# Moving the values' projection and the keys' transposes in the TensorE order of a linear-attention and low-rank FFN block

## The reference

```
xn  = layernorm(layernorm(x))*ln_g + ln_b          # attention: second norm with weights
q, k, v = split(xn @ W_qkv + b_qkv)
gate = sigmoid(layernorm(x) @ W_gate + b_gate);  gate = gate / (mean(gate) + EPS)
q = relu(q*gate)**2 + EPS;   k = relu(k*gate)**2 + EPS
out_t = (q_t . sum_{s<=t} k_s v_s^T) / (q_t . sum_{s<=t} k_s + EPS)      # per head
x = x + out @ W_proj + b_proj
P = layernorm(x) @ U1;  H = gelu(P @ V1 + b1);  x = x + (H @ U2) @ V2 + b2   # rank 128, width 2048
```

## Time and profile before

| | us |
|---|---|
| median of 3 runs (lowest, highest) | 1736.85 (1735.19, 1737.18) |
| the profiled execution's own time | 1734.75 |
| its span in the profile | 1733.0 |
| PE busy in the span | 1703.1 (98%) |
| DVE busy | 1340.5 (77%) |
| POOL busy | 894.4 (52%) |
| ACT busy | 671.5 (39%) |

### The profile page before, as it was taken

One profiled execution on the slowest core, in us unless ns is written; L12 is line 12 of the kernel. 1 busy time (PEld: TensorE's weight loads), 2 busy tenths in 40 slices (PEclk: granted clock), 3 DMA queues, 4 the chain that ended last, 5 costly groups with the idle time before them and its releaser, 6 DMA issues.

```text
span 1733.0 us, 39458 instructions
## 1 busy us (share of the span) xinstructions
PE 1703.1 (98%) x16477; PEld 1429.5 (82%) x16477; DVE 1340.5 (77%) x2159; ACT 671.5 (39%) x1242; POOL 894.4 (52%) x1026
## 2 busy tenths in 40 slices
PE   6999999999999999999999999999999999999997
PEld 4788888888888888888888888888888888888886
DVE  6877877777877777777778778778777778777775
ACT  4243343443433343433433434434333434334333
POOL 4365555555555545555555555555555555555540
PEclk9999999999999999999999999999999999999999
DMA  7111111111011111110111110111111111101100
GB/s 220 59 35 53 34 53 40 33 53 53 33 53 33 41 53 40 46 53 23 52 53 34 53 44 30 53 53 33 53 39 36 53 41 45 53 23 52 41 20 26
DMA packets 61937, 82.09 MB, mean 47 GB/s; under 512 B 14952, under 2 KB 25600, under 8 KB 61760
## 3 DMA queue, kind: packets, MB, share of 16 engines
q1 hardware_dynamic: 60896, 77.99, 14.3%
q10 hardware_dynamic: 864, 1.57, 0.3%
HBM read 62.60 MB, written 16.94 MB: 46 GB/s over the span
## 4 chain that ended last, share of the span: by engine, by line
PE 95%; DVE 3%; ACT 0%; issue 0%; DMA 0%; POOL 0%; SPq 0%; DVEq 0%; POOLq 0%
PE ps_a L825 11%; PE ps_a L826 10%; PE ps_a L827 10%; PE scores L825 8%; PE scores L827 7%; PE scores L826 7%; PE ps_h L825 6%; PE scores L832 5%; PE ps_h L826 4%; PE ps_h L827 4%; PE scores L960 4%; PE scores L995 4%; PE ps_q L825 3%; PE ps_q L827 3%; PE ps_q L826 3%; PE scores L989 2%
## 5 line engine op out<-in xcount | busy, mean ns | idle before, releaser
L432 POOL TENSOR_TENSOR h_lo<-h_full,h_hi 128x512 fp32r<-128x512 f32 x244 | 334.1, 1379 | 194.7 <-DVE h_hi L654 194.7
L825 PE MATMUL ps_a<-wx_hi,zt_hi 128*128 128x512 f32 x768 | 312.7, 407 | 6.3 <-DVE key_sums L765 4.2
L827 PE MATMUL ps_a<-wx_hi,zt_lo 128*128 128x512 f32 x768 | 305.2, 397 | 0.0
L826 PE MATMUL ps_a<-wx_lo,zt_hi 128*128 128x512 f32 x768 | 305.2, 397 | 0.0
L515 ACT ACTIVATE h_full<-ps_h,cols 128x256 f32<-128x256 f32 x512 | 213.6, 472 | 21.2 <-PE ps_h L827 19.5
L654 DVE CAST h_hi<-h_full 128x512 fp32r<-128x512 f32 x256 | 173.8, 698 | 39.7 <-ACT h_full L515 39.7
L452 POOL TENSOR_TENSOR key_lo<-keys,key_hi 128x512 fp32r<-128x512 f32 x64 | 83.3, 1301 | 191.4 <-ACT key_hi L550 191.4
L825 PEld LDWEIGHTS ps_a<-wx_hi,zt_hi 128*128 128x128 f32 x768 | 145.8, 190 | 39.0 <-DVE zt_lo L609 7.1
L827 PEld LDWEIGHTS ps_a<-wx_hi,zt_lo 128*128 128x128 f32 x768 | 145.3, 189 | 35.5
L526 ACT ACTIVATE query_t<-scores 128x512 f32<-128x512 f32 x64 | 38.3, 598 | 346.2 <-PE scores L832 346.2
L720 DVE TENSOR_TENSOR probs<-scores,causal 128x2048 f32<-128x2048 f32 x64 | 146.7, 2292 | 32.5 <-PE scores L960 32.5
(11 more groups left out here) (158 smaller groups left out, 4225.6 us busy)
## 6 DMA issues: line engine op xcount, KB each, us to landing
xs<-L_attn_x SPq DMA_DIRECT2D x64, 256.0 KB, 4.0
out<-x1s SPq DMA_DIRECT2D x64, 256.0 KB, 2.1
xt<-x_turned SPq DMA_DIRECT2D x63, 256.0 KB, 4.2
key_sums<-carry_rows SPq DMA_DIRECT2D x60, 256.0 KB, 3.8
rows<-turned_rows SPq DMA_DIRECT2D x63, 64.0 KB, 4.4
x1s<-L_attn_W_gate SPq DMA_DIRECT2D x4, 256.0 KB, 4.1
x1s<-L_ffn_U SPq DMA_DIRECT2D x4, 256.0 KB, 6.5
carry_rows<-key_sums SPq DMA_DIRECT2D x64, 2.0 KB
```

Source lines behind the costliest of these rows:

```text
L432: E.tensor_tensor(h_lo[:, i % SLOTS, :], h_full[:, i % SLOTS, :], h_hi[:, i % SLOTS, :].bitcast(F32), ALU.subtract).then_inc(s["h_lo_ready ...
L825: E.matmul(ps, wh, mh, start=start and i == 0, stop=False)
L826: E.matmul(ps, wh, ml, start=False, stop=False)
L827: mm = E.matmul(ps, wl, mh, start=False, stop=stop and i == last)
```

## The change

Three things move. On PE the transposes of the keys leave their place behind QUERY, where they turned the keys of c; now they turn the keys of n, a step ahead, behind the product of probabilities and values, and write to `ps_a` instead of `ps_t`. VALUE comes directly behind the scores in both kinds of step; in an odd step the first FFN product used to stand between them. Behind VALUE or around it the FFN products are regrouped in twos: in an odd step pairs 0 and 1 stand between VALUE and the state's update, and pairs 2 and 3 behind the key transposes; in an even step pairs 4 and 5 stay ahead of the scores and 6 and 7 stand behind the key transposes. The key sums move behind pair 3 (or 7). ACT's and DVE's lists follow.

```
                 if n.exists:
                     pe.wait_ge(s["gate_evac"], n.done())
                     project(QUERY, ps_a, s["query_done"])
-                if c.exists:
-                    if d.exists:
-                        pe.wait_ge(s["x1t_ready"], d.done())
-                    else:
-                        pe.wait_ge(s["query_t_ready"], c.done())
-                    pe.wait_ge(s["key_ready"], c.done())
-                    transpose4(keys[:, c.half, :], s["tk_done"])
...
                     pe.wait_ge(s["key_t_ready"], c.done())
+                    pe.wait_ge(s["query_t_ready"], c.done())
+                    if d.exists:
+                        pe.wait_ge(s["x1t_ready"], d.done())
...
                     mm.then_inc(s["scores_done"], 1)
-                if ffn.exists and b % 2:
-                    h_pair(ffn, pairs[0])
                 if n.exists:
...
                     project(VALUE, ps_a, s["value_done"])
+                if ffn.exists and b % 2:
+                    h_pair(ffn, pairs[0])
+                    h_pair(ffn, pairs[1])
...
                     mm.then_inc(s["ot_done"], 1)
+                if n.exists:
+                    pe.wait_ge(s["value_ready"], n.done())
+                    pe.wait_ge(s["key_ready"], n.done())
+                    transpose4(keys[:, n.half, :], s["tk_done"], ps_a)
                 if ffn.exists:
-                    h_pair(ffn, pairs[1 if b % 2 else 2])
+                    h_pair(ffn, pairs[2])
+                    h_pair(ffn, pairs[3])
                 if n.exists:
-                    pe.wait_ge(s["value_ready"], n.done())
+                    pe.wait_ge(s["key_t_ready"], n.done())
                     pe.wait_ge(s["key_lo_ready"], n.done())
                     E.matmul(ps_a[:, :], causal_r[:, :], key_hi[:, :], start=True, stop=False)
                     E.matmul(ps_a[:, :], causal_r[:, :], key_lo[:, :], start=False, stop=True)\
                         .then_inc(s["sums_done"], 1)
-                if ffn.exists:
-                    if b % 2:
-                        h_pair(ffn, pairs[2])
-                    h_pair(ffn, pairs[3])
```

More of the change, by code:

```diff
@@ L538, in step @@
                         .then_inc(s["x1t_hi_ready"], 1)
-                if c.exists:
-                    act.wait_ge(s["tk_done"], c.done())
-                    E.activation(key_t[:, :, :].rearrange(flat), ps_t[:, :], ACT.Copy)\
-                        .then_inc(s["key_t_ready"], 1)
                 if b % 2 and ffn.exists:
@@ L551, in step @@
                 if ffn.exists:
-                    gelu(ffn, pairs[0 if b % 2 else 1])
+                    if b % 2:
+                        gelu(ffn, pairs[0])
+                    gelu(ffn, pairs[1])
                 if c.exists:
@@ L556, in step @@
                         .then_inc(s["ot_hi_ready"], 1)
+                if n.exists:
+                    act.wait_ge(s["tk_done"], n.done())
+                    E.activation(key_t[:, :, :].rearrange(flat), ps_a[:, :], ACT.Copy)\
+                        .then_inc(s["key_t_ready"], 1)
+                if ffn.exists:
+                    gelu(ffn, pairs[2])
                 z_head(Chunk(p, b + 1))
                 if ffn.exists:
-                    if b % 2:
-                        gelu(ffn, pairs[1])
-                    gelu(ffn, pairs[2])
                     gelu(ffn, pairs[3])
@@ L746, in step @@
                                     ALU.add).then_inc(s["state_ready"], 1)
+                if ffn.exists and b % 2:
+                    h_head(ffn, pairs[1], finishing)
                 if c.exists:
```

21 lines of the change are left out of this document (10 added, 11 removed).

## The result

| | before | after |
|---|---|---|
| median of 5 runs each (lowest, highest), us | 1736.85 (1735.19, 1737.46) | 1726.7 (1723.25, 1727.78) |
| the profiled execution's own time | 1734.75 | 1725.1 |
| its span | 1733.0 | 1723.4 |

What follows compares the result with a forecast made beforehand. PE bounds the kernel, busy 1703.1 of 1733.0 us. Bubbles 4.8, switches 0, last step 2.7 and first steps 0.6 make 8.1 us off 1734.75, 1726.7; the median lies 2.1 above, 1728.8, range 1721.5 to 1738.

Steps and rivals of the forecast that it cites:

- The bubble: Odd step, last FFN product waiting for the gelu two products before: this gap of 0.15 to 0.16 us goes, 4.8 us.
- The switch from tiles to transposes: Transposes directly behind the tiled products: the switch costs 0.10 us, so the swap is worth 0 per step.
- rival (a): The switch from tiles to transposes is free, or the clock holds: 6.2 or 1.2 us more gain, to 1721.4; chance 0.15.
- The last step: Last step with scores: two FFN products fill the wait for x1t_lo, scores start 2.2 to 3.3 us earlier, taken as 2.7.
- the case at half clock: Last step: the two FFN products take 2.8 us, so the scores start at 1693.2, the 2.2 us end of the gain.
- The first steps: Scores of the third step can go earlier, less 0.25 us paid in the second waiting for key_t: 0.6 us gained together.
- The clock at the start: Work behind PE's 4.2 us wait may leave half clock: 1.2 us at most, left out of the sum, in the range.
- `value_ready` 0.2 to 1.0 us ahead of its need: Even step: DVE's values end 0.2 to 1.0 us before the transposes behind the product of probabilities need them.
- Rival (c): POOL's key_lo precedes DVE's queries operation, value_ready is late in 31 even steps: 15.5 us less 8.1, 1744; chance 0.17.
- Key sums' chain, x1t, ot: Key sums have 0.6 us to spare for key_t, ot is done before the output projection, the x1t_ready wait can only shrink.
- P's halves get a whole projection more: Odd step: P's halves, which the first FFN product just met, get a whole projection more time with VALUE earlier.

Runs made afterwards that it cites:

- regroup_only: The changed kernel with the transposes of keys back behind QUERY, in bank ps_t: 1731.6 us, ratio 0.9973 to the kernel before.
- gelu_first: The kernel before with the odd step's second gelu and its cast taken ahead of zt, PE's list untouched: 1740.38 us, ratio 1.0027.
- warm: The changed kernel with matmuls that nobody reads filling PE's waits at the start and in the last step with scores: 1724.61 us, ratio 0.9940.
- joined_warm: The changed kernel with the edits of joined and warm together: 1724.47 us, ratio 0.9938 to the kernel before.
- one_pad: The changed kernel with only an unused buffer of 32 bytes per partition ahead of zt_hi: 1718.29 us, ratio 0.9901 to the kernel before.
- delay2: The changed kernel with two unread DVE operations ahead of values in each even step, their buffer shifting later ones by 64 bytes: 1727.4 us, ratio 0.9955.
- value_back: The changed kernel with the odd step's VALUE back behind the first FFN product: 1737.09 us, ratio 1.0008 to the kernel before.
- pads_on_after: The changed kernel with 32 unused bytes ahead of zt_hi and 32 more ahead of x1t_hi: 1709.35 us, ratio 0.9851 to the kernel before.
- joined: The changed kernel with the even step's transposes of queries moved directly ahead of those of the normed rows: 1725.69 us, ratio 0.9941.
- pads_and_fill: pads_on_after with unread matmuls in the two waits of the last step with scores: 1708.87 us, ratio 0.9846 to the kernel before.

## Why the prediction was right, point by point

It said 1728.8 us in a range of 1721.5 to 1738.0, faster; measured 1726.7. By its own steps:

- **The bubble, 29 x 0.16 + 0.15 = 4.8 us**: right. regroup_only measures 29 x 0.153 = 4.4 us in the middle, where 4.6 were forecast. It works as told, by distance between a product and the gelu two before it; gelu_first removes it by moving that gelu. The forecast 1.42 us for the last two products of the odd step was 1.50, since they now stand behind transposes (0.08), which the same paragraph's next one had said.
- **The switch from tiles to transposes, 0.10, so that the swap is worth 0**: a mis-sized term. The transposes take 0.41 behind the tiles against 0.35 elsewhere: 0.06, between the forecast and rival (a). Against regroup_only the moved transposes save 0.055 and 0.036 us in the two kinds of step, 2.6 us in 58 steps. The choice of the row with the same neighbour ahead was the better of the two ends, but what follows the tiles matters too. The Trainium skill's TensorEngine Tiling (Array Packing), Key Properties, by which a change of mode drains TensorE, agrees with both rows (0.11 into a product, 0.06 into transposes); it gives no size.
- **The last step, 2.7 us**: the step that failed. The order of events was right (the scores start as soon as the two products are through), but they came 1.5 us earlier, under the 2.2 of the case at half clock: the transposes of the normed rows ahead started 0.3 us later behind their GATE (30.86 against 30.56) and took 0.69 us, where warm has 0.41, at half clock too. Then "everything after hangs on the scores" took the work behind them at its old pace, and it ran at half clock where before it had run at full: 0.86 us for the product of probabilities alone, 1.4 for all up to the output projection. The end gave 0.2 us. warm shows the clock as the cause: with PE kept busy the 2.7 us appear. The scores were to start near 1687.3 and started at 1684.37, because their GATE came 9.5 us earlier, where the forecast gave the steps ahead of it 5.4.
- **The first steps, 0.6 us**: the fifth GATE came 2.3 us earlier in the profile, but this differs by execution: profiles of three kernels with the old order have it at 109.59 to 110.61 (mean 109.96), seven with the new order (warm and joined_warm, which fill the start, left out) at 108.14 to 110.14 (mean 109.26). The difference, 0.7, doesn't contradict 0.6 and doesn't prove it. The waits for `key_t` were there as said, but in three steps, 2.1 us together, and not 0.25 in one.
- **The clock at the start, left in the range with 1.2 us at most**: it goes with most of the difference among those profiles. In the changed kernel's profile the second GATE starts at 39.69 at half clock, and from 42.70 its distances are 0.24 or less, at full clock; in one_pad, with the same order, all twelve are at half clock: they start at 39.64, and the next work starts at 44.90 instead of 43.87. That is 1.1 us, by execution and not by the order. Of the seven, the three whose clock is full again before 43 us have the fifth GATE at 108.14 to 108.42, the four where it is full only after 44.6 us at 109.81 to 110.14. The changed kernel's profile is one of the three, the one of the kernel before is of the slower sort (full again at 46.2).
- **`value_ready` 0.2 to 1.0 us ahead of its need**: right, at the upper end: 1.0. The casts took 0.76 for both. **Rival (c)** did not come: the queries' operation took 0.69 us, and POOL's `key_lo` started 0.35 behind it (799.60 to 799.25), where 0.5 had been walked. Its two halves are shown apart: gelu_first and `zt_lo` show the exclusion, and delay2 that a `value_ready` past the room is paid, 0.2 us in each even step.
- **Key sums' chain, x1t, ot**: none of them has a wait in the 58 steps.
- **What the walk did not look for**: that the two moves need each other (value_back). It holds in the prediction's favour, since VALUE's "P's halves get a whole projection more" stands there, but as a side remark; it is the condition of the whole change.

The same window near the start, in the changed kernel's profile and then in one_pad's (the third number from the right is the granted clock):

```profile
42.90:44.50 1.60, 1.60 (x10) 1.33 (x9) 1.60 (x4) 0.00 (x0) 0.00 (x0) 1.00 0.00 0
```

```profile
42.90:44.50 1.60, 1.60 (x6) 1.21 (x5) 1.60 (x4) 0.00 (x0) 0.00 (x0) 0.50 0.00 0
```

Sum of the measured parts: 4.2 + 2.6 + 0.3 in the middle, 2.3 at the start and 0.2 at the end are the 9.6 us of span. That the forecast's 8.1 was near is in part luck: a term too low (0 for 2.6) and a term too high (2.7 for 0.2) nearly cancel. By the means of the profiles about 1.6 us of the start is chance of one execution.

## What to carry to other kernels

When PE is the bound and has no long waits, the gaps of 0.05 to 0.2 us at the seams between kinds of work are what an order can win; read them as distances between starts, and look behind each moved block for what it had been covering. A forecast for the ends of a program has to ask after each new or remaining idle stretch at which clock the next work runs, and to carry both answers, since here it differed between executions of one order. And compare a kernel with another only with their buffers at the same addresses, or measure what a shift of 32 bytes does alone: here one such shift was worth 7 to 8 us and two were worth more than the change, and an added scratch buffer would have been read as a gain of an added operation.

## What the runs showed of the hardware

- The pace of matmuls depends on where their operands lie in SBUF. 32 bytes of shift made 12 matmuls of 128x512 take 2.75 instead of 2.80 us and 24 of 128x256 take 2.87 instead of 2.84 (one_pad against the changed kernel); 64 bytes made the latter 2.80 (delay2, pads_on_after). Which pair of operands does it, and by what rule of addresses, stays open: only these shifts were tried, and always of several buffers together.
- A block of four transposes costs 0.08 us behind it, ahead of a projection, an FFN product or another such block (joined), and leaving the tiles costs 0.06 into transposes and 0.10 to 0.11 into a product of the full array.
- DVE's subtraction of 128x512 took 1.82 instead of 0.7 us when POOL's started 0.02 us ahead of it. The Trainium skill, SBUF — State Buffer, Who interferes with whom, has this rule, and gelu_first is a case in which it turns the bubble's gain of 0.13 us per odd step into a loss of as much, 3.8 us in the 58 steps.
- The same order with the same idle stretch of 2.4 us ahead ran at granted clock 0.50 in the changed kernel's profile and at 1.00 in one_pad's; with matmuls in that stretch (warm, pads_and_fill) it was 1.00.
